# A two-layer cross-attention kernel on one core: the first 85 microseconds are put in another order

## What is computed

```python
# _L0_xattn_ref, with query = layernorm(x), key = value = ctx_1024
q = einsum('bld,ed->ble', query, Wq) + bq
k = einsum('bkd,ed->bke', key, Wk) + bk
scores = einsum('bqe,bke->bqk', q, k) / 32
x = x + softmax(scores) @ value
# then: linear attention, feed-forward (3 cycles), a second cross-attention on the
# same context, low-rank attention with 16 heads, attention plus 8-expert MLP
```

## Time and profile before

| | before |
|---|---|
| median of 3 runs | 556.14 us |
| profiled execution, span from the first to the last instruction | 557.0 us |
| PE busy | 518.1 us (93%) |
| DVE busy | 355.3 us (64%) |
| ACT busy | 286.3 us (51%) |
| POOL busy | 72.5 us (13%) |
| mean granted TensorE clock | 0.992 |

### The profile page before, as it was taken

One profiled execution on the slowest core, in us unless ns is written; L12 is line 12 of the kernel. 1 busy time (PEld: TensorE's weight loads), 2 busy tenths in 40 slices (PEclk: granted clock), 3 DMA queues, 4 the chain that ended last, 5 costly groups with the idle time before them and its releaser, 6 DMA issues.

```text
span 557.0 us, 9530 instructions
## 1 busy us (share of the span) xinstructions
PE 518.1 (93%) x3615; PEld 358.4 (64%) x3615; DVE 355.3 (64%) x849; ACT 286.3 (51%) x623; POOL 72.5 (13%) x64
## 2 busy tenths in 40 slices
PE   7899999899999898999989999899999999988992
PEld 5556564465666564557645678688888788774551
DVE  3885546975546864447364747888889788654235
ACT  2687871626843127575246845888876553021110
POOL 0114141200000000000001220133310111200001
PEclk9999999999999999999999999999999999999997
DMA  8786572000000000000140021022339005960001
GB/s 264 257 255 113 98 146 60 1 1 1 1 0 1 1 29 0 2 0 1 46 181 2 2 98 55 11 69 76 76 115 393 9 1 169 348 241 0 1 1 38
DMA packets 45197, 44.06 MB, mean 79 GB/s; under 512 B 18656, under 2 KB 41184, under 8 KB 45024
## 3 DMA queue, kind: packets, MB, share of 16 engines
q1 hardware_dynamic: 45152, 43.45, 25.8%
HBM read 38.73 MB, written 0.52 MB: 70 GB/s over the span
## 4 chain that ended last, share of the span: by engine, by line
PE 62%; DVE 18%; issue 11%; ACT 6%; POOL 2%; DMA 1%; SPq 0%; DVEq 0%; ACTq 0%; POOLq 0%
PE ps L654 9%; PE ps L683 7%; PE ps L809 6%; PE ps L793 6%; PE ps L668 4%; PE ps L685 4%; PE ps L968 3%; PE ps L993 3%; PE ps L778 2%; PE ps L715 2%; PE ps L766 2%; PE ps L503 2%; DVE mx L1600 1%; ACT arena L1157 1%; ACT arena L1142 1%
## 5 line engine op out<-in xcount | busy, mean ns | idle before, releaser
L654 PE MATMUL ps<-ctx_tr,qtl 128*128 128x512 f16 x384 | 90.7, 379 | 0.7 <-DVE qtl L1493 0.5
L1157 ACT ACTIVATE arena<-ps 128x512 f32<-128x512 f32 x64 | 38.0, 596 | 51.6 <-PE ps L654 51.3
L1600 DVE TENSOR_REDUCE mx<-arena 128x1 f32<-128x512 f32 x64 | 43.2, 682 | 32.2 <-ACT arena L1157 31.6
L654 PEld LDWEIGHTS ps<-ctx_tr,qtl 128*128 128x128 f16 x384 | 36.8, 98 | 38.7 <-issue 1.4
L683 PE MATMUL ps<-ctx_nat,pth 128*128 128x512 f16 x172 | 58.2, 379 | 0.0
L1142 ACT ACTIVATE arena<-arena,small 128x512 f32<-128x512 f32 x64 | 45.8, 715 | 8.2 <-DVE small L1609 8.2
L809 PE MATMUL ps<-arena,ctx_tr 128*128 128x256 f16 x384 | 47.2, 273 | 0.1
L685 PE MATMUL ps<-ctx_nat,ptl 128*128 128x256 f16 x172 | 46.9, 273 | 0.0
L668 PE MATMUL ps<-const,arena 128*128 128x128 f32 x256 | 39.2, 276 | 7.2 <-ACT arena L1142 6.2
L1614 DVE TENSOR_TENSOR ptl<-ps,pth 128x512 f16<-128x512 f32 x43 | 29.5, 688 | 21.7 <-ACT pth L1150 21.6
L1346 POOL TENSOR_TENSOR rstd<-mv,col 128x2 f32<-128x2 f32 x13 | 9.9, 765 | 248.6 <-DVE mv L1453 248.6
(11 more groups left out here) (300 smaller groups left out, 1039.6 us busy)
## 6 DMA issues: line engine op xcount, KB each, us to landing
ctx_nat<-in_w_e SPq DMA_DIRECT2D x8, 1024.0 KB, 7.8
ctx_tr<-in_w_e SPq DMA_DIRECT2D x6, 1024.0 KB, 11.8
work<-in_ctx SPq DMA_DIRECT2D x8, 512.0 KB, 4.7
ctx_tr<-in_ctx SPq DMA_DIRECT2D x8, 512.0 KB, 7.6
work<-in_w_vo SPq DMA_DIRECT2D x8, 512.0 KB, 3.8
ctx_nat<-in_w_l SPq DMA_DIRECT2D x4, 512.0 KB, 5.3
arena<-in_w_e SPq DMA_DIRECT2D x2, 1024.0 KB, 7.5
wts<-in_rows SPq DMA_DIRECT2D x1, 1024.0 KB, 5.1
```

The costliest lines, as they stand in the source:

```text
L654: mm = pe.matmul(ps[:, n % 2, :], qtl[:, qh, d, u * P:(u + 1) * P], CT[:, t0:t0 + KT, kh, d, :], start=(i == 0 and d == 0), stop=(i == 2 a ...
L1157: act.activation(S[:, n % SRING, :], ps[:, n % 2, :], ACT.Copy).then_inc(s("score_copied"), 1)
L1600: dve.tensor_reduce(mx[:, u, c:c + 1], S[:, n % SRING, :], AX.X, ALU.max).then_inc(s("score_max"), 1)
```

## The change

- SP no longer issues `cols` and the weights. ScalarE does, as its first three instructions: `cols` (semaphore `col_in`), Wq (`wx_in`), Wk (`wk_in`). Each user waits for its own.
- VectorE's row statistics of batch 0 come first; -0.5 is a constant set on the chip (`minus_half`), and the small scalars made from `cols` come behind `prep_out(0)`.
- GpSimd cuts the low halves of all 16 chunks; `cut_lo` is gone from VectorE. Its power for batch 1 stands ahead of chunk 10 (`X1_AT`).
- ScalarE cuts high halves one place earlier (`g + 2`), and both copies of chunk 1 are VectorE's (`TURNED_BY_DVE`).
- 24 busy matmuls in place of 40, and 6 more behind the first transposes (`OPENING`).
- Batch 1's projection moves from steps 0 to 8 of the list to steps 8 to 17, and its banks from 4, 5, 7 to 2, 3, 7; the turns then need no wait for it (`qt_lo`).
- Late in the kernel two semaphores get other names (`m_sub8`, `m_exp8` become counts of `m_sub`, `m_exp`), with the same instructions before and behind them.

```diff
-POOL_CUTS = NCH
+X1_AT = 10
+OPENING = (24, 6)
+TURNED_BY_DVE = (1,)
...
-            (2, 5, 6, 9, 15,),
-            (1, 1, 6, 13, 16,),
-            (1, 2, 6, 10, 16,),
+            (16, 17, 20, 23, 33,),
+            (18, 22, 27, 34, 34,),
+            (16, 17, 19, 24, 29,),
...
-    return (4, 5, 6) if (what, b) == ("a", 1) else (4, 5, 7) if what == "x" or (what, b) == ("l", 1) else (2, 3, 7)
+    return (4, 5, 6) if (what, b) == ("a", 1) else (4, 5, 7) if (what, b) in (("x", 0), ("l", 1)) else (2, 3, 7)
...
-            sp.dma_start(col[:, :], cols).then_inc(s("const_in"), 16)
-            sp.dma_start(wx, w_x).then_inc(s("wx_in"), 16)
...
-                    pe.wait_ge(s("const_in"), 32)
+                    pe.wait_ge(s("const_in"), 16)
...
                 pe.wait_ge(s("qT"), k + 1)
+                if k == 0:
+                    pe.wait_ge(s("wk_in"), 16)
                 bk = COL[what + "_bk0"]
...
-                else:
-                    pe.wait_ge(s("qt_lo"), B)
...
-            keep_busy(40, 0)
+            keep_busy(OPENING[0], 0)
...
-            for _ in range(4):
+            for _ in range(3):
...
+            keep_busy(OPENING[1], 0)
+            next(first)
...
             def prep_out(g):
+                if g in TURNED_BY_DVE:
+                    return
                 act.wait_ge(s("ctT_ps"), g + 1)
...
-                        if g + 1 < NG:
-                            cut_hi(g + 1)
+                        if g + 2 < NG:
+                            cut_hi(g + 2)
...
             C = lambda name, n=P: col[0:n, COL[name]:COL[name] + 1]
-            act.wait_ge(s("const_in"), 32)
+            act.dma_start(col[:, :], cols).then_inc(s("col_in"), 16)
+            act.dma_start(wx[:, 0], w_x[:, 0]).then_inc(s("wx_in"), 16)
+            act.dma_start(wx[:, 1], w_x[:, 1]).then_inc(s("wk_in"), 16)
+            act.wait_ge(s("col_in"), 16)
             act.activation(becol, C("beta"), ACT.Exp).then_inc(s("becol"), 1)
             act.wait_ge(s("becol"), 1)
-            act.wait_ge(s("halves"), 1)
             cut_hi(0)
...
             prep_out(0)
+            cut_hi(2)
             for _ in project("x", 0):
                 pass
+            act.wait_ge(s("halves"), 1)
             side0, attention1 = chain(linear_attention(0), feed_forward(0), project("y", 0)), linear_attention(1)
...
-            pool.wait_ge(s("const_in"), 32)
-            for b in range(B):
-                layernorm("x", b)
-            for g in range(POOL_CUTS, NG):
+            nh = minus_half.broadcast_to([P, 2])
+            pool.wait_ge(s("ones_set"), 2)
+            layernorm("x", 0)
+            for g in range(NG):
+
+                if g == X1_AT:
+                    layernorm("x", 1)
...
-                if g == POOL_CUTS:
-                    pool.wait_ge(s("ctx_lo"), g)
...
-            def cut_lo(g):
-                if g >= POOL_CUTS:
-                    return
-                dve.wait_ge(s(loaded(g)[0]), loaded(g)[1])
-                dve.wait_ge(s("ctx_hi"), g + 1)
-                dve.tensor_tensor(CN[:, g * KT:(g + 1) * KT, 1, :], stage[slot_of(g)], CN[:, g * KT:(g + 1) * KT, 0, :],
-                                  ALU.subtract).then_inc(s("ctx_lo"), 1)
-
...
-                dve.tensor_copy(CT[:, g * KT:(g + 1) * KT, 1].rearrange("p t c k -> p t (c k)").bitcast(U32),
-                                ps[:, 3, :].bitcast(U32).rearrange("p (t k) -> p t k", t=KT)).then_inc(s("ctT_lo"), 1)
+                for h in (0, 1) if g in TURNED_BY_DVE else (1,):
+                    dve.tensor_copy(CT[:, g * KT:(g + 1) * KT, h].rearrange("p t c k -> p t (c k)").bitcast(U32),
+                                    ps[:, 2 + h, :].bitcast(U32).rearrange("p (t k) -> p t k", t=KT))\
+                        .then_inc(s("ctT_hi" if h == 0 else "ctT_lo"), 1)
...
-                        if g + 1 < NG:
-                            cut_lo(g + 1)
...
             dve.memset(ones[:, :], 1.0).then_inc(s("ones_set"), 1)
-            dve.wait_ge(s("const_in"), 32)
+            dve.memset(tenth, 0.1)
+            dve.memset(minus_half, -0.5).then_inc(s("ones_set"), 1)
+            first = project("x", 0)
+            next(first)
+            dve.wait_ge(s("const_in"), 16)
             dve.tensor_copy(ident16[:, :], ident)
-            dve.memset(tenth, 0.1)
+            next(first)
+            next(first)
+            dve.wait_ge(s("col_in"), 16)
+            next(first)
+            prep_out(0)
             dve.tensor_scalar(b4h, C("cn_b4"), 0.5, None, ALU.mult)
...
             dve.tensor_scalar(b3h, C("gc_b3"), 0.5, None, ALU.mult).then_inc(s("halves"), 1)
-            first = project("x", 0)
-            for _ in range(3):
-                next(first)
-            cut_lo(0)
-            next(first)
-            prep_out(0)
-            cut_lo(1)
             for _ in first:
```

18 lines of the change are left out of this document (8 added, 10 removed).

## The result

The changed kernel took 561.15 us (median of 4 runs, 560.14 to 562.58) beside 556.29 for the kernel before: ratio 1.0085 [1.0067, 1.0104]. In a second set of rounds it was 560.87 beside 556.69, ratio 1.0064 [1.0041, 1.0087]. The forecast was 552.8. The profiled execution after has a span of 558.3 us and took 560.14.

What follows compares the result with a forecast made beforehand. PE was taken to bound all but the first 46 us, so gains could only come there. 2.9 + 5.8 - 4.8 - 0.5 = 3.4, rounded down to 3.3, from the median 556.14 gave 552.8 us, range 550.9 to 555.7.

Steps and rivals of the forecast that it cites:

- Start to first scores: Opening up to batch 0's first scores: 17.1 us in place of 20.00, 2.9 gained, with chunk 0 at 8.6.
- From L511 to the scores took 4.25: End of the opening: the 4.25 us from L511 to the scores were kept, L511 at 12.9, scores at 17.1.
- The span was 557.0, 0.9 above the median: Base of the sum: the profile's span set beside the median, and the gain taken from the median, 556.14 us.
- First scores to first turn: Rounds ahead of the first turn: 20.8 us in place of 26.56, 5.8 gained, as batch 1's pieces leave.
- rival B: Rounds before the first turn: keep the old 2.95 us as ScalarE's cuts wait for loads; 2.7 us, 555.5; chance 0.13.
- First turn to batch 1's scores: Stretch behind the first turn, 37.39 us before: 4.8 us of batch 1's PE work come back, plus 0.5 of waits.
- the 0.5: Behind the first turn: new waits at ScalarE's first turned copy and VectorE's half step 29, between 0 and 2.5 us.
- rival C: Behind the first turn: VectorE's hold at half step 29 makes tile 0's second half 2 us late; 554.8; chance 0.07.
- VectorE's own cuts, the only large operations with two inputs in SBUF, go: GpSimd's cuts beside VectorE: argument that they do not collide over shared SBUF interfaces and keep 2.12 to 2.13 us.
- Rival D: GpSimd's cuts, all chunks: each lengthened by waiting for a VectorE operation, 2.13 + 1.2 us; 557.7; chance 0.05.
- rival A: Opening, `prep(0)` and Wk products: low clock falls where not covered, 1.25 + 0.6 us; 554.7; chance 0.12.
- Each is shorter: Opening: argument against the low clock; PE's two gaps, 5.0 to 6.6 and 10.0 to 11.85, each shorter than before's.

Runs made afterwards that it cites:

- the kernel with the wait: Changed kernel, with GpSimd starting chunk 10's cut only when VectorE has scaled batch 1's x: 556.04 us, ratio 1.0001 to before; again 556.60, 0.9991.

## Why the forecast was wrong

**Start to first scores, forecast 17.1 with 2.9 gained: 0.1 gained profile to profile, 1.0 lost at like clock.** The steps up to the Wq product came true (3.58 and 7.93 for 3.7 and 8.1). Chunk 0 was put at 8.6; it came at 9.59 in the profile after, and over fourteen profiles at 7.94 to 9.59, median 8.66, with an issue 0.94 earlier. So 8.6 was right as a middle value and 1.0 off in this profile. The rule of the Trainium skill, "DMA: Bandwidth & Descriptors", section "Issuing engines are not separate DMA queues", that only issue time is saved, had given 9.5 in the forecast's working. The profile after agrees with that, the thirteen others are earlier, and with 8.64 and 9.55 for the later issue of before they neither bear the rule out nor refute it. Two things failed. The first is "From L511 to the scores took 4.25". Where GpSimd waits, the same products (now L513) start at 12.89, for a forecast of 12.9, and the scores 5.11 behind them, at 18.00: the small scaling is held (1.39 for 0.17), and TensorE waits 1.38 for 0.52. The second is the base, 3 us too late. GpSimd's slower cut, 2.13 for 1.23 on VectorE, was noted ("VectorE's place in this is lost") and priced right. But the kernel before at full clock has its scores at 16.95, so there was no gain for it to lessen. The gain of 2.9 was the difference between a good execution of the new kernel and a bad one of the old, in which `cols` came 1.66 later and the clock was low. "The span was 557.0, 0.9 above the median" compared a span with a device time; the two differ by 1.7 to 2.2.

**First scores to first turn, forecast 20.8: 21.08.** Right, with rounds of 2.5 (ScalarE's copies L1138 start at 22.82 and five rounds later at 35.38); GpSimd alone kept up with them, and no wait of ScalarE there names a DMA, so rival B is not seen.

**First turn to batch 1's scores, forecast 4.8 lost and 0.5 of new waits: 44.32 after 37.39, 6.9 lost.** The projection cost 4.3. The step that failed is the 0.5. I looked for waits behind ScalarE's first copy and behind VectorE's half step 29, where PE lost nothing that the waits show (rival C not seen), and not at the scaling at half step 17, because I had ruled out collisions with GpSimd: "VectorE's own cuts, the only large operations with two inputs in SBUF, go". The rule I quoted has two halves, two SBUF inputs or a two-port mode. The runs show that VectorE's TENSOR_SCALAR from SBUF to SBUF in float32, with one tensor as input, is held too, at 128x256 and at 128x2: 2.2 us for 0.41 and 1.39 for 0.17, and 0.16 with the input in PSUM. The Trainium skill names the operation, on a page that the forecast did not use: "SBUF — State Buffer", section "Who interferes with whom", lists `tensor_scalar` among those that can enter a 2-port mode and then take the pair of SBUF ports shared with GpSimd, the later of the two blocked for the whole instruction of the other. The trace agrees that both sizes are held until a cut ends; which mode they ran in no run here shows. The profile before could have warned of a hold, but not of this one. Beside GpSimd's cut from 42.21 to 44.34 stand two small operations of VectorE between SBUF tiles, both 128x1. The second, L1609, has two inputs and took 0.39, for 0.16 elsewhere. The first is a TENSOR_SCALAR and kept its usual 0.21:

```profile
43.72 0.21 DVE L1606 TENSOR_SCALAR small<-small 128x1 f32<-128x1 f32 x1
```

No TENSOR_SCALAR of two or more columns stood beside a cut there. Rival D had the right pair of engines, and lengthened the wrong one: GpSimd's cuts stayed at 2.13 to 2.18.

**The low clock, rival A at 0.12.** It was priced at 1.9 and given for the opening only. At L517 it cost 1.6 in the profile (3.53 for 1.97), of which 0.8 is left at the first scores (10.29 us from the cut of chunk 0, for 9.47), since the late small scaling is then not held; and in one profile of two it cost more behind the collision, a gap that the forecast did not know. "Each is shorter" was no argument: the gap ahead of chunk 0's turn was 3.13 in the first profile, longer than the 2.30 of before, and 2.14 in the second, shorter, and the clock fell behind both.

**The account.** At like clock: 5.47 gained to the first turn, 4.30 lost to the projection, 1.05 lost in the opening, together 0.1 gained, and the kernel with the wait is equal to before (0.9991 and 1.0001). The collision costs 2.63, and the two scalings took 4.33 in both profiles of the changed kernel. From the profile with the wait, span 553.8, an estimate for it at full clock is then 556.4; its ten executions had 557.6 to 560.8. In the two that were profiled the rest closes: 558.3 has 1.06 for the later landing of chunk 0 and 0.82 for the low clock in the opening; 560.0 has 0.08 for the landing, 1.44 in the opening, 0.33 in the rounds and 1.68 behind the collision. So 2.6 of the measured 4.2 to 4.9 is the collision, shown by the edit that removes it, and the rest is mostly low clock, read from two profiles and not from the eight others. Why the clock falls behind a gap in one execution and not in the next is open. So are 0.4 us behind the power, 470.8 for 470.4, in the three kernels in which VectorE cuts chunk 0 at the right place.

## What to carry to other kernels

Before one profile becomes the base of a sum, compare its device time, not its span, with the median; where a clock or a landing makes executions differ, read the stretch in two profiles. When work is moved to GpSimd, list every VectorE operation that then runs beside it: here those with an input in PSUM passed (0.16), and float32 TENSOR_SCALAR between SBUF tiles did not at 128x256 and 128x2, though it did at 128x1. The price is what is left of GpSimd's operation, and in some executions the clock as well, if TensorE waits. Moving 4.3 us of TensorE work from a stretch where it is busy 22.94 of 26.55 us to one where it is fully busy changed nothing; taking one slow cut and one held operation off the way to the first scores gave 0.3% against the kernel with the wait and 0.4% against the kernel before.

## What the runs showed of the hardware

- Two operations of VectorE in a row were each held by one cut, in all three profiles with the collision (the changed kernel's two and the one with more busy matmuls): in the first the second of GpSimd's cuts started at 44.0, ahead of VectorE's second scaling, so that 0.73 us of work took 4.33.
- The hold shows as duration of the held instruction, not as idle time before it; only min and max of a line tell it (405 and 2205 ns).
- Size mattered at the lower end: float32 TENSOR_SCALAR between SBUF tiles was held beside a cut at 128x2 in all eight profiles where they met (1.02 to 1.40 us for 0.17), and at 128x1 in none (0.21 in five profiles, 0.14 in others).
- The granted clock fell to 0.50 behind idle times of TensorE of 3.1 us (10 to 13 us, first profile of the changed kernel) and 2.14 (10 to 12 us, second), and behind 2.4 us (44 to 46.4) in the second only. Behind 2.16 us in the kernel with the wait, and behind the same 2.4 in the first profile, it kept 1.00. The length of the gap alone did not decide it.
- In three of sixteen profiles, one of them of the kernel before, it fell between 487 and 497 us, where TensorE idled 0.6 and 0.3 us, and this cost 1.2 to 1.3 us.
